# A graph layer, a mixing layer and a feed-forward layer on one core: key/value products moved to the front, a deeper look-ahead, a third build bank, fewer stores

## The reference

```
xn  = layernorm(x)
deg_out, deg_in = sums of edge_weight by source and by target
norm = edge_weight * rsqrt(deg_out[src] * deg_in[dst] + 1e-12)
h6  = relu(segment_sum((xn @ W6)[src] * norm, dst) + b6)
h7  = relu(segment_sum((h6 @ W7)[src] * norm, dst) + b7)
gnn = h7 @ Wp + bp
q, k, v = xn @ wq.T, xn @ wk.T, xn @ wv.T        # 4 heads of 64
k, v = layernorm per head of k and of v (gain and offset each)
kv  = einsum('bhsd,bhse->bhde', k, v) / 6250     # one 64x64 matrix a head
mix = (q @ kv) @ wo.T + bo
x   = x + gnn + mix
x   = x + ffn(layernorm(x))                      # 2 of 8 experts, chosen once for all rows
```

## Time and profile before

| | us |
|---|---|
| median of 3 runs | 3768.78 (3760.32 to 3772.62) |
| the profiled execution | 3763.83 |
| its span, first to last instruction | 3762.0 |
| TensorE / GpSimd / VectorE / ScalarE busy | 2974.0 / 2162.5 / 1794.8 / 1136.8 |

### The profile page before, as it was taken

The page is one execution under the profiler, slowest core; times in us unless marked ns, Lnnn a source line. Parts: engine busy times, 40 slices in busy tenths (PEclk is TensorE's granted clock), DMA queues, the critical chain, the costliest instruction groups (busy, mean ns, idle before and its releaser), DMA issues.

```text
span 3762.0 us, 52448 instructions
## 1 busy us (share of the span) xinstructions
PE 2974.0 (79%) x16152; PEld 2012.6 (53%) x16152; DVE 1794.8 (48%) x4526; ACT 1136.8 (30%) x4013; POOL 2162.5 (57%) x2090
## 2 busy tenths in 40 slices
PE   4565468878888888888885488788897887878998
PEld 4454335555555556555553256466565554655666
DVE  9999745556565555655542131322411244222334
ACT  6787453334443433433330010200100111002211
POOL 5776566666666666666664666566665666630000
PEclk8788869989999999999987689899898988998999
DMA  4210134445444444444445545455555554543221
GB/s 125 63 35 2 26 108 140 138 127 156 144 133 152 146 132 148 144 137 142 140 140 162 143 142 187 124 186 182 152 189 186 172 157 146 175 145 110 76 78 47
DMA packets 254147, 492.54 MB, mean 131 GB/s; under 512 B 61871, under 2 KB 135487, under 8 KB 253525
## 3 DMA queue, kind: packets, MB, share of 16 engines
q0 software_dynamic: 88704, 243.35, 22.8%
q1 hardware_dynamic: 158657, 239.29, 19.3%
q10 hardware_dynamic: 6500, 6.40, 0.5%
HBM read 376.56 MB, written 112.35 MB: 130 GB/s over the span
## 4 chain that ended last, share of the span: by engine, by line
PE 52%; DVE 17%; issue 10%; another core or an unknown queue 6%; ACT 4%; DMA 3%; POOL 3%; DVEq 2%; SPq 2%; ACTq 1%; POOLq 0%
PE ps L678 22%; PE ps L656 9%; DVE ab L1060 6%; PE ps L847 5%; PE ps L640 5%; PE ps L860 4%; DVE ab L1058 3%; POOL ringb L1908 2%; DMA ab<-in_x 2%; ACT ab L1683 1%; PE ps L603 1%; PE ps L619 1%; SPq L1969 1%; DVE mlb L1237 1%
## 5 line engine op out<-in xcount | busy, mean ns | idle before, releaser
L1908 POOL DMA_INDIRECT ringb<-t,src x1848 | 1852.5, 1002 | 1056.3 <-issue 487.8
L678 PE MATMUL ps<-xb,ab 125*128 125x256 f32 (+1 forms) x4700 | 1199.8, 399 | 85.8 <-issue 74.9
L678 PEld LDWEIGHTS ps<-xb,ab 125*128 125x128 f32 x4700 | 918.0, 199 | 336.9 <-issue 178.1
L656 PE MATMUL ps<-mlb 128*125 128x300 f32 x1260 | 482.5, 472 | 190.9 <-ACT side L1687 99.3
L1683 ACT ACTIVATE ab<-ps 125x250 f32 x724 | 293.6, 405 | 633.0 <-PE ps L656 366.0
L640 PE MATMUL ps<-ringb,Sb 128*32 128x257 f32 (+1 forms) x3696 | 334.4, 421 | 119.7 <-DVE Sb L1201 47.9
L656 PEld LDWEIGHTS ps<-mlb 128*125 128x125 f32 x1260 | 225.2, 203 | 351.2 <-issue 303.2
L562 PE MATMUL ps<-ab 128*50 128x125 f32 x3228 | 243.8, 304 | 184.9 <-ACT ab L1610 126.1
L1270 DVE TENSOR_TENSOR ab<-ab,side 125x50 f32 x724 | 177.8, 246 | 400.7 <-ACT side L1687 197.2
L1881 POOL TENSOR_TENSOR ab<-ab,wn 128x100 f32<-128x100 f32 x201 | 274.1, 1368 | 128.1 <-DVE ab L1058 128.1
L562 PEld LDWEIGHTS ps<-ab 128*50 128x50 f32 x3228 | 204.0, 142 | 224.5 <-DVE ab L1060 192.9
(11 more groups left out here) (227 smaller groups left out, 2681.2 us busy)
## 6 DMA issues: line engine op xcount, KB each, us to landing
ad<-ab SPq DMA_DIRECT2D x210, 312.5 KB
ab<-ad SPq DMA_DIRECT2D x210, 312.5 KB
ringb<-t,src POOLq DMA_INDIRECT x1848
x2t<-mlb SPq DMA_DIRECT2D x13, 500.0 KB
xb<-x2t SPq DMA_DIRECT2D x13, 500.0 KB, 8.3
xb<-in_x SPq DMA_DIRECT2D x10, 625.0 KB
t<-xb SPq DMA_DIRECT2D x10, 625.0 KB
kvb<-t SPq DMA_DIRECT2D x50, 125.0 KB
```

Source lines behind the costliest of these rows:

```text
L656: e.matmul(PS[(2, 7, 4, 5)[bank_of(t)]][0:R, 0:HR], low[:, slot_of(t), :], high[:, slot_of(t), :], start=True, stop=True).then_inc(s_bld, 1)
L678: ins = e.matmul(PS[3][:, 0:wd], lhs, X[0:R, k, 0:wd], start=k == 0, stop=k == NT - 1)
L1908: e.indirect_dma_start(msg[:, slot * QT + k, 0:width], None, table, bass.IndirectOffsetOnAxis(src[:, t:t + 1], 0)).then_inc(s_g[slot], 16)
```

## The change

**Key/value products in the front.** The transposes and the product are issued between the front's batches: KV_AT gives tile i the batch 20 + 3.6 i. TensorE transposes from the normalised rows in SBUF after that batch, and multiplies two batches later. ScalarE copies the transposes one batch after the first, and the raw product two batches after that. SP stores both to DRAM, one batch on (kvd is new). Layer 0 loads the raw products (125 x 512 a tile) and does the rest as before, a phase earlier. The centering moves to batch 17.

**One-hots two steps ahead.** VectorE makes in step s the one-hots of step s+2, into three groups of slots (HG), and adds the first columns of step s-2. ScalarE scales the low one-hots of s+1 ahead of all evictions of s. `side` has nine places instead of six, the tables' registers three sets. Dense products start a step later. The clearing of A moves to the third step of its chunk; ScalarE's first eviction takes over the waits for TensorE and the stores, and waits for the clearing only at tile 15.

**Three build banks.** Builds of layer 0 use banks 2, 7 and 5 in turn.

**Two stores.** SP stores a finished A in two transfers of 125 x 3200, in steps 1 and 4 of the next chunk, instead of ten of 125 x 640 in steps 0 to 9.

```diff
+HG = 3
+MLW = 3940
+FRONT_EX = 2400
+LATE_CLEAR = 15
-SD = 6
+SD = 9
+SA = 2
+SW = AP_ // SA
+KV_AT = [20 + i * 18 // 5 for i in range(NT)]
+T1_AT = [19 + 9 * b for b in range(NB)]
-        MULT_AT[0].setdefault((_d + 1) * PD + 1 + _k * (PD - 2) // NT, []).append((_d, _k))
+        MULT_AT[0].setdefault((_d + 1) * PD + 2 + _k * (PD - 2) // NT, []).append((_d, _k))
...
         def bank_of(t):
-            return t % 2 + 2 * (t >= tile_of(DY))
+            return (4, 5)[t % 2] if t >= tile_of(DY) else (2, 7, 5)[t % 3]
...
         def pe_program(e):
+            def kv_transposed(i):
+                e.wait_ge(s_nx, i + 1)
+                if i >= 1:
+                    e.wait_ge(s_kxc, i)
+                for h in range(2):
+                    ins = e.transpose(PS[4][:, h * P:h * P + R], X[0:R, i, h * P:(h + 1) * P], ident[0:R, 0:R])
+                ins.then_inc(s_ktr, 1)
+
+            def kv_product(i):
+                e.wait_ge(s_kxc, i + 1)
...
+                if i >= 1:
+                    e.wait_ge(s_krc, i)
+                for h in range(2):
+                    ins = e.matmul(PS[5][0:R, :], xT[:, i % 2, h, :], wkv[:, h, :], start=h == 0, stop=h == 1)
+                ins.then_inc(s_kmm, 1)
...
+                if c in KV_AT:
+                    kv_transposed(KV_AT.index(c))
+                if c - 2 in KV_AT:
+                    kv_product(KV_AT.index(c - 2))
...
-                if t >= 2:
-                    e.wait_ge(s_ev, t - 1)
+                n = banks(t)
+                if t >= n:
+                    e.wait_ge(s_ev, t - n + 1)
...
-                    if (s + 1) % PD == 0 and 1 <= (s + 1) // PD < DY:
-                        clear((s + 1) // PD)
-                    for t in BUILD_AT[0].get(s - 1, ()):
+                    if s % PD == 2 and 1 <= s // PD < DY:
+                        clear(s // PD)
+                    for t in BUILD_AT[0].get(s - 2, ()):
                         first_column(t)
-                    hots(s + 1)
+                    hots(s + 2)
...
+            def kv_rows(i):
+                k = i % 2
+                e.wait_ge(s_ktr, i + 1)
...
+                e.activation(xT[:, k, :, :], PS[4][:, 0:2 * P].rearrange("p (h c) -> p h c", h=2)[:, :, 0:R],
+                             ACT.Copy).then_inc(s_kxc, 1)
+
+            def kv_raw(i):
+                k = i % 2
+                e.wait_ge(s_kmm, i + 1)
...
+                e.activation(raw[0:R, k, :], PS[5][0:R, :], ACT.Copy).then_inc(s_krc, 1)
...
+                if k == 0 and 2 <= d < DY:
+                    e.wait_ge(s_mul, 5 * (d - 1))
+                    e.wait_ge(l_as[place], 16 * SA * loads_of(d - 1, place))
+                if k == LATE_CLEAR and d < DY:
+                    e.wait_ge(s_az, d + 1)
...
-                    for t in BUILD_AT[0].get(s, ())[:1]:
-                        evict(t)
                     weigh_lo(s + 1)
-                    for t in BUILD_AT[0].get(s, ())[1:]:
+                    for t in BUILD_AT[0].get(s, ()):
                         evict(t)
...
-                if s % PD < PA and 1 <= s // PD <= DY:
-                    store_A(s // PD - 1, s % PD)
+                if s % PD in (1, 4) and 1 <= s // PD <= DY:
+                    store_A(s // PD - 1, s % PD // 4)
...
-    nc = bacc.Bacc("TRN2", target_bir_lowering=False, num_devices=1)
+    nc = bacc.Bacc("TRN2", target_bir_lowering=False, num_devices=1, dynamic_dma_scratch_size=8192)
```

More of the change, by code:

```diff
@@ L470, in loads_of @@
             return (n + 1 - parity) // 2
[L472 to L478, removed]
         def builds_before(s):
@@ L584, in kv @@
                     ins.then_inc(s_kk, 1)
[L585 to L597, removed]
-                    if i == 0:
-                        e.wait_ge(s_cen, 3)
-                    if i >= 1:
-                        e.wait_ge(s_kv, 5 * i - 2)
-                    for h in range(2):
-                        ins = e.matmul(PS[5][0:R, :], xT[:, k, h, :], wkv[:, h, :], start=h == 0, stop=h == 1)
-                    ins.then_inc(s_kmm, 1)
             def hidden(i, s, slowly):
@@ L1095, in dve_program @@
             e.wait_ge(l_wts, 16 * N_WTS)
[L1096 to L1103 removed]
+            for k in range(2):
+                e.wait_ge(l_xs[k], 16 * loads_of(NT, k))
+                e.wait_ge(l_kr[k], 16 * loads_of(NT, k))
             e.wait_ge(s_hz, 1)
@@ L1357, in dve_program @@
                 hots(0)
+                hots(1)
                 load_next(0, -1)
@@ L1945, in sp_program, with kv_stored @@
                     e.dma_start(X[0:R, LNB * b + 2 * LNB:LNB * b + 3 * LNB, 0:D], blocks(x)[b + 2]).then_inc(l_x[b % 2], 16)
+            def kv_stored(i):
+                k = i % 2
+                e.wait_ge(s_kxc, i + 1)
+                e.dma_start(xtd[i // 4].rearrange("p (h n) -> p h n", h=2)[:, :, i % 4 * R:(i % 4 + 1) * R],
+                            xT[:, k, :, :]).then_inc(l_xs[k], 16)
+                e.wait_ge(s_krc, i + 1)
+                e.dma_start(kvd[i * R:(i + 1) * R, :], raw[0:R, k, :]).then_inc(l_kr[k], 16)
+            for c in range(len(BATCHES)):
+                if c in T1_AT:
+                    rows_stored(T1_AT.index(c))
+                if c - 4 in KV_AT:
+                    kv_stored(KV_AT.index(c - 4))
             e.wait_ge(s_rsd, 3)
@@ L1952, in kv_load @@
                 if i == 0:
-                    e.wait_ge(l_t1, 16 * NB)
+                    for j in range(2):
+                        e.wait_ge(l_kr[j], 16 * loads_of(NT, j))
                     e.wait_ge(s_st, 16)
                 if i >= 2:
-                    e.wait_ge(s_ktr, i - 1)
-                e.dma_start(xt[0:R, k, :], tile_rows(t1, i)).then_inc(l_kx[k], 16)
+                    e.wait_ge(s_kv, 5 * (i - 2) + 3)
+                e.dma_start(kin[0:R, k, :], kvd[i * R:(i + 1) * R, :]).then_inc(l_kx[k], 16)
             def store_A(d, p):
```

145 lines of the change are left out of this document (78 added, 67 removed).

## The result

The changed kernel takes 3737.27 us (median of 6 runs, 3735.65 to 3739.61) against 3766.24 before (6 runs): a ratio of 0.9916, 95% interval 0.9888 to 0.9944. It is faster, by 29 us. The forecast was 3625, with 3580 to 3680 as its range, and 3737 lies outside it.

What follows compares the result with a forecast made beforehand. The prediction took no engine as full: layer 0's engines wait for each other, 6.50 us a step above all floors. 3763.8 us less 156 (layer 0) plus 16 (front) gave 3624, forecast as 3625, range 3580 to 3680.

Steps and rivals of the forecast that it cites:

- The front's coupling: Front: ScalarE waits for TensorE, which at times waits for GpSimd; 13 us taken, between zero and 49.
- It just fits: Front: ScalarE's two added copies, 0.98 us a tile, fit into its 1.01 us free in 3.6 batches.
- Less two thirds of 0.64 for the builds: Layer 0: the look-ahead removes two thirds of TensorE's 0.64 us a step at builds, towards 5.7 a step.
- the ring's slack: Layer 0: engines wait for each other in a ring with one step of slack, at 6.50 us a step.
- 178.0 us more passes between back-to-back issues: Layer 0: added to 727.6 us of GpSimd gathers, giving a floor of 5.15 us a step.
- The first: Rival, layer 0: GpSimd becomes the bound, 5.20 us a step, total 3501 us; chance 0.12.
- The second: Rival, layer 0: look-ahead gives nothing, VectorE's chain bounds, a step stays at 6.02 or little over, 3700 us; chance 0.20.
- a step over 6.0 fells the look-ahead: Sign, layer 0: a measured step above 6.0 us would show that the look-ahead fails.
- The third: Rival, front: it becomes TensorE's at a low clock, +250 us, total 3858 us; chance 0.06.
- six tenths of the front: Front: TensorE's low clock level (1.2 GHz) decides once it holds for over this share.
- The fourth: Rival, gathers: the smaller descriptor ring holds them up, each 0.17 us longer, +314 us, total 3938 us; chance 0.02.
- The fifth: Rival, layer 0: the chunk's new late start eats what the rest gives, total 3764 us; chance 0.05.

Runs made afterwards that it cites:

- copy_later: The changed kernel with ScalarE's copy of the raw product in the front one batch later: 3495.16 us, ratio 0.9802 to the kernel before.
- spread: The changed kernel with the front's transposes copied two batches after them, product three after, raw copy five after: 3478.10 us, ratio 0.9797 to the kernel before.
- the first pair: The kernel before and the changed kernel as first measured and traced: 3766.24 and 3737.27 us, ratio 0.9916.
- the second pair: The kernel before and the changed kernel, both without edits, run and traced again later: 3559.20 and 3519.78 us, ratio 0.9880.
- dve_more: The changed kernel with two small clearings on VectorE added in each step of layer 0, each waited for: 3525.53 us, ratio 0.9917 to the kernel before.
- pool_more: The changed kernel with two small clearings on GpSimd added ahead of each step's gathers in layer 0: 3626.25 us, ratio 1.0181 to the kernel before.

## Why the prediction was wrong, step by step

**The direction and the fixed parts** were right: faster; the clearing with almost no waits (27.3 to 4.5 us); GpSimd's waits for the sums well down (172.2 to 27.5); TensorE loses the key/value work; layer 1 unchanged (1315 and 1320 us from step 243 to the last gather); the stores worth nothing.

**The front's coupling, forecast 13 us with the centering's 2.6 beside it, measured 57 in all.** The step that failed is "It just fits". I summed ScalarE's work (0.98 us into 1.01 free) and took 13 us for its waits without placing the product in time. The working was there: TensorE's 1.06 for the batch and some 2 us of product behind it, against the one ScalarE batch of 1.47 us that the order puts between. That is 1.6 us of waiting, 50 times, as far as nobody else is late in the same batches. copy_later and spread show that it is this spacing and not the amount of work: the same instructions fit in VectorE's 1.75.

**Layer 0, forecast 5.70 a step, measured 6.03.** Two steps failed here, a wait that was misread and a floor that was too low. "Less two thirds of 0.64 for the builds" took TensorE's 113.4 us before builds as the ring's slack, which a look-ahead removes. In the first pair 96.6 of them stayed; in the second, without stalls, they were 59.5 and fell to 18.7. So about half of the 113.4 came with the stalls: the "remote" waits of the earlier trace rows that I left unread. The first pair's steps are longer by 6.50 - 5.97 = 0.53 us before (5.97 is the second pair's value for the same 176 steps) and by 6.05 - 5.43 = 0.62 after. Even without them the gain is 0.44, not 0.71, because the floor was too low: "178.0 us more passes between back-to-back issues" counts only the gathers that waited for nothing else. Each gather needs its pass of 0.30 us, so four take 4 x (1.033 + 0.30) = 5.33 and not 5.15, and 5.40 was reached, at 1.051 a gather. That 5.15 seemed borne out by the 5.20 of the steps without builds was chance: their gathers are shorter (0.96 us in the second pair). The two parts then share the 0.45 between 5.86 and 5.40.

**The sum of two gains.** I priced the product at the 0.48 that a step gains when key/value work stops, and the look-ahead on top of it. Each is there alone, at less than its price (0.36 and 0.35 measured); added up they would go below the floor, and both together bring 0.44.

**The rivals.** The first (GpSimd's floor) named the bound but put it 0.2 us too low, and its 3501 took 3 us for the front and left out the stalls. The second's size for layer 0 (6.02 a step) is what the first pair gave, and its reason is refuted: VectorE is not the bound (dve_more), and alone the look-ahead brings 77 us, both on later chips without the stalls. So my sign "a step over 6.0 fells the look-ahead" misled: 6.03 came, and the look-ahead works. The third, a front slowed by TensorE's clock, went the other way: the granted clock of the front rose from 0.84 to 0.93, with 1.00 from 388 to 453 us, while TensorE's busy time there rose from 245.5 of 448 us to 343.9 of 505. Its "six tenths of the front" doesn't follow from its own figures either: at the full clock it has TensorE at 6.3 us beside VectorE's 6.3, so any share at the low level would have made TensorE the longer. The fourth, the smaller ring, is refuted: in the second pair a gather takes 946 ns in the median before and 949 after, and in the first pair its mean is 1002 and 1003. The fifth, that nothing comes of it, is excluded by the interval, which ends at 0.9944.

**What stays open** is what the stalls of the first pair are. No kernel here took them away or made them. The record doesn't name the chip of the first pair, so whether they come from a chip or from the state it was in at that time wasn't shown either. That they explain the longer steps rests on the account of GpSimd's idle time, not on an experiment.

## What to carry to other kernels

Moving work to a stage with idle time pays only where the receiving order leaves enough time between producer and consumer: add up the producer's chain behind the last common wait, not the work, and put the consumer that far behind. Work out the floor of the busiest in-order queue with the pass of every instruction in it before adding up gains, and price each part alone and with the others; here the look-ahead, which cost nothing, would have brought 73 us alone, and the whole change brought 40. A row that looks like slack (TensorE before its builds) can hold a stall of another cause. Waits that end at a releaser which the trace can't name belong in the account: here neither order won them back (0.55 us a step before, 0.61 changed).

## What the runs showed of the hardware

GpSimd's indirect gathers run as a stream with 0.30 us between two of them, even where they wait for nothing else: beside the builds a gather takes 1.05 us (5.40 for four with the passes), in the 12 steps without builds 0.96 (5.06 for four). More work on GpSimd shows in full (pool_more, 0.45 us a step).

The same program took 3766 us in the first pair and 3560 in the later runs. The front is 448.1 and 448.2 us, and from the last gather to the end it is 428 us in both; the difference lies between the first gather and the last (2885.6 and 2684.6 us), in the steps shown 1144.8 and 1051.5 us for 176.

A second build in each step on TensorE, 70 us more busy time, and 71 us more on VectorE in 176 steps, left layer 0 as long as it was.
